# Digits of a packed adjacency taken three to a shift, and an early sum in half-width columns from tile 5

## The reference

```
def layer0(x):                        # GRU over summed messages
    msg = x[src] @ W_msg.T + b_msg + edge_embed[clip(edge_type, 0, 8)]
    m = segment_sum(msg, dst)
    h = gru_cell(m, x, W_ih, W_hh, b_ih, b_hh)
def layer1(x):                        # two mean-aggregation layers
    h = relu(x @ w_self1 + mean_agg(x) @ w_neigh1 + b1)
    y = h @ w_self2 + mean_agg(h) @ w_neigh2 + b2
x1  = layernorm(x + layer0(x))
out = layernorm(x1 + layer1(x1))
```

## Time and profile before

| | us |
|---|---|
| median of 3 runs (783.27 to 784.06) | 783.52 |
| the profiled execution | 783.98 |
| its span | 782.2 |
| PE busy, share of the span | 673.8, 86% |
| DVE busy | 505.3, 65% |
| ACT busy | 272.9, 35% |
| POOL busy | 159.9, 20% |
| mean granted TensorE clock | 0.971 |

### The profile page before, as it was taken

One profiled execution on the slowest core, in us unless ns is written; L12 is line 12 of the kernel. 1 busy time (PEld: TensorE's weight loads), 2 busy tenths in 40 slices (PEclk: granted clock), 3 DMA queues, 4 the chain that ended last, 5 costly groups with the idle time before them and its releaser, 6 DMA issues.

```text
span 782.2 us, 15765 instructions
## 1 busy us (share of the span) xinstructions
PE 673.8 (86%) x3184; PEld 317.7 (41%) x3184; DVE 505.3 (65%) x1614; ACT 272.9 (35%) x701; POOL 159.9 (20%) x339
## 2 busy tenths in 40 slices
PE   2777777777888989999988999967999999999995
PEld 0222222222333433434333444433555555766663
DVE  7999969999899999999997245661111111034434
ACT  3665552223333534544458325451101112100000
POOL 2454324232222222222220002221001111100000
PEclk9999978999999999999999999989999999999998
DMA  5000000000000000000001011101001110121110
GB/s 152 0 0 0 1 0 1 0 0 1 0 1 0 1 1 0 1 1 1 1 0 52 28 34 34 41 15 44 27 14 40 40 40 28 58 70 41 53 45 16
DMA packets 29312, 17.25 MB, mean 22 GB/s; under 512 B 1737, under 2 KB 28101, under 8 KB 29278
## 3 DMA queue, kind: packets, MB, share of 16 engines
q1 hardware_dynamic: 29278, 16.78, 7.3%
HBM read 10.36 MB, written 6.42 MB: 21 GB/s over the span
## 4 chain that ended last, share of the span: by engine, by line
PE 53%; DVE 25%; issue 10%; DVEq 7%; ACT 3%; DMA 1%; POOL 0%; ACTq 0%; POOLq 0%; SPq 0%
DVE S L585 12%; PE PS L938 11%; PE PS L1175 10%; PE PS L867 9%; PE PS L828 5%; DVE D L579 4%; PE PS L1106 3%; DVE digits L574 3%; DVEq L585 2%; PE PS L999 2%; PE PS L1140 2%; DVEq L606 1%; PE PS L1094 1%; PE PS L1095 1%; ACT AT L1217 1%
## 5 line engine op out<-in xcount | busy, mean ns | idle before, releaser
L867 PE MATMUL PS<-S,D 128*128 128x449 bf16 x786 | 222.8, 368 | 61.3 <-DVE S L585 54.4
L585 DVE TENSOR_SCALAR S<-iota_h,src_col,src_w 128x440 bf16<-128x440 f16 x747 | 250.6, 388 | 0.0
L1217 ACT ACTIVATE AT<-digits 128x512 int32 (+5 forms) x200 | 103.7, 519 | 174.1 <-DVE digits L574 174.1
L867 PEld LDWEIGHTS PS<-S,D 128*128 128x128 bf16 x786 | 75.7, 96 | 208.1 <-DVE S L585 184.6
L438 POOL COPY S<-T 128x27 bf16 (+1 forms) x264 | 109.7, 417 | 241.0 <-PE PS L867 227.1
L579 DVE TENSOR_TENSOR D<-iota_t,dst 128x384 bf16<-128x384 f16 x262 | 91.3, 349 | 12.8 <-PE PS L867 12.1
L828 PE MATMUL PS<-AT,xp 128*128 128x512 bf16 x375 | 89.4, 379 | 0.8 <-ACT Cn L1206 0.8
L938 PE MATMUL PS<-AT,x1p 128*128 (+2 forms) x450 | 86.1, 348 | 0.2 <-issue 0.2
L1175 PE MATMUL PS<-xp,AT 128*128 128x384 bf16 (+1 forms) x525 | 85.6, 326 | 0.0
L574 DVE TENSOR_SCALAR digits<-packedT 128x512 int32<-128x512 int32 (+1 forms) x200 | 62.0, 360 | 11.0 <-ACT packedT L1211 9.3
L1175 PEld LDWEIGHTS PS<-xp,AT 128*128 (+2 forms) x525 | 51.5, 98 | 33.9 <-issue 0.3
(11 more groups left out here) (155 smaller groups left out, 620.0 us busy)
## 6 DMA issues: line engine op xcount, KB each, us to landing
slot<-x_rows SPq DMA_DIRECT2D x12, 256.0 KB, 3.0
xstage<-x SPq DMA_DIRECT2D x6, 256.0 KB, 5.3
x_rows<-slot SPq DMA_DIRECT2D x6, 256.0 KB, 2.2
y_rows<-slot SPq DMA_DIRECT2D x6, 256.0 KB, 2.2
res_rows<-slot SPq DMA_DIRECT2D x6, 256.0 KB, 2.5
slot<-res_rows SPq DMA_DIRECT2D x6, 256.0 KB, 2.8
out_rows<-slot SPq DMA_DIRECT2D x6, 256.0 KB, 2.2
slot<-xT SPq DMA_DIRECT2D x3, 256.0 KB, 2.7
```

The lines of the kernel that those rows point to most:

```text
L585: v.tensor_scalar(S[:, u, 0:SPAN], iota_h[:, :], src_col[:, ds(c0 + u, 1)], src_w[:, ds(c0 + u, 1)], ALU.is_equal, ALU.mult).then_inc(sem( ...
L867: mm(PS[:, par, 0:WIDE], ring[:, u, :], S[:, u, 0:WIDE], start=opens and u == 0, stop=last).then_inc(sem("tiles_summed" if last else "item ...
L1217: a.activation(AT[:, f:f + n // P * DIGITS - DIGITS + 1:DIGITS, ds(t * P, w)], digits[:, at:at + n].rearrange("p (g m) -> p g m", m=P)[:, ...
```

## The change

VectorE takes three words a tile in place of eight digits. Word w is the packed integer shifted right by 3w and masked with three fields of 3 bits, at bits 0, 9 and 18. They lie in the bytes 0, 1 and 2 of the int32, shifted in their byte by 0, 1 and 2 bits. So `take_digits` has three operations (shift and mask as before, another constant), with no ring of planes: word w of the next tile is written once all stores of the tile before are done. It is called once a tile, where the first share stood. ScalarE's `store_digits` reads bytes with a step of four: three copies, one for each byte lane, of 3, 3 and 2 digits (3 x 384, 3 x 384, 2 x 384 elements), scaled by 1, 1/2 and 1/4, and a fourth for the 25th source tile (128 elements). Each stores a sum for `count`, and the count of stores in the semaphore goes from 8 to 4 a tile.

TensorE's early sums of the first 2048 columns are cut in eight sums of 256 columns (`early_half`), each over two tiles, 2u + 5 and 2u + 6, in tiles 5 to 20: 12, 12 and 15 matmuls in odd tiles, 12, 12 and 12 in even ones. Two such sums share a bank; `early_agg` counts after the second. The fifth sum of 512 stays as it was. Nothing is changed in the passes after.

```diff
-SHARES = ((0, 1, 2), (3, 4, 5), (6, 7))
-LEAST = len(SHARES)
+LEAST = 3
...
-RING = 4
-PLANES = TURNED + (RING - 1) * MAIN
+WORDS = 3
+LANES = 3
+STORES = LANES + 1
+MASK = sum(((1 << BITS) - 1) << (BITS * WORDS * lane) for lane in range(LANES))
...
-EARLY_CUTS = (0, 7, 13, 19, TILES)
+EARLY_CUTS = (0, 13, TILES)
...
-            def take_digits(t, some):
+            def take_digits(t):
 
                 dve.wait_ge(sem("packedT_in"), t + 1)
-                for f in some:
-                    dve.wait_ge(sem("digits_stored"), t * DIGITS + (f + 1 + DIGITS - RING))
-                    at, n = plane(f)
-                    v.tensor_scalar(digits[:, at:at + n], packedT[:, 0:n], BITS * f, (1 << BITS) - 1, ALU.logical_shift_right,
+                dve.wait_ge(sem("digits_stored"), t * STORES + STORES)
+                for word in range(WORDS):
+                    n = MAIN if word else TURNED
+                    v.tensor_scalar(digits[:, word, 0:n], packedT[:, 0:n], BITS * word, MASK, ALU.logical_shift_right,
                                     ALU.bitwise_and).then_inc(sem("digits_taken"), 1)
...
-                    edge_rows(t + n, (LAG + n) % 2, lambda i: take_digits(t + n - LAG, SHARES[i]))
+                    edge_rows(t + n, (LAG + n) % 2, lambda i: i or take_digits(t + n - LAG))
...
+            def early_half(u, j0, j1):
+
+                pe.wait_ge(sem("digits_stored"), (2 * u + 3) * STORES)
+                if j0 == 0:
+                    pe.wait_ge(sem("x_split"), NC + 1)
+                at = u % 2 * 2 * P
+                for j in range(j0, j1):
+                    for s in range(PARTS):
+                        ins = mm(PS[:, EARLY_BANKS[u // 2], at:at + 2 * P], xp[:, j, s, :], AT[:, j, u * 2 * P:(u + 1) * 2 * P],
+                                 start=(j == 0 and s == 0), stop=(j == TILES - 1 and s == PARTS - 1))
+                if j1 == TILES and u % 2:
+                    ins.then_inc(sem("early_agg"), 1)
+
             def early_piece(t, n):
-                q, r = divmod(t - LAG - 4, 4)
-                if 0 <= q < EARLY:
+                u, r = divmod(t - LAG - 2, 2)
+                if 0 <= u < 2 * EARLY:
                     j0, j1 = EARLY_CUTS[r:r + 2]
-                    early_sum(q, j0 + (j1 - j0) * n // LEAST, j0 + (j1 - j0) * (n + 1) // LEAST)
+                    early_half(u, j0 + (j1 - j0) * n // LEAST, j0 + (j1 - j0) * (n + 1) // LEAST)
...
-            def store_digits(t, w, some=range(DIGITS)):
-                for f in some:
-                    act.wait_ge(sem("digits_taken"), t * DIGITS + f + 1)
-                    at, n = plane(f)
-                    a.activation(AT[:, f:f + n // P * DIGITS - DIGITS + 1:DIGITS, ds(t * P, w)],
-                                 digits[:, at:at + n].rearrange("p (g m) -> p g m", m=P)[:, :, 0:w], ACT.Copy,
-                                 accum_out=count[:, ds(t, 1), f:f + 1].rearrange("p a b -> p (a b)")).then_inc(sem("digits_stored"), 1)
+            def store_digits(t, w):
+                digit_bytes = digits[:, :, :].bitcast(u8).rearrange("p f (g m k) -> p f g m k", m=P, k=4)
+                for lane in range(LANES):
+                    n = min(WORDS, DIGITS - WORDS * lane)
+                    act.wait_ge(sem("digits_taken"), t * WORDS + n)
+                    a.activation(AT[:, 0:TILES - 1, ds(t * P, w)].rearrange("p (g f) m -> p f g m", f=DIGITS)[:, WORDS * lane:WORDS * lane + n, :, :],
+                                 digit_bytes[:, 0:n, 0:GROUPS, 0:w, lane], ACT.Copy, scale=2.0 ** (8 * lane - BITS * WORDS * lane),
+                                 accum_out=count[:, ds(t, 1), lane:lane + 1].rearrange("p a b -> p (a b)")).then_inc(sem("digits_stored"), 1)
+                a.activation(AT[:, TILES - 1, ds(t * P, w)], digit_bytes[:, 0, GROUPS, 0:w, 0], ACT.Copy,
+                             accum_out=count[:, ds(t, 1), LANES:LANES + 1].rearrange("p a b -> p (a b)")).then_inc(sem("digits_stored"), 1)
...
-                    for share in SHARES:
-                        store_digits(t - LAG, P, share)
+                    store_digits(t - LAG, P)
```

More of the change, by code:

```diff
@@ L46 @@
 ROW = WIDE + -WIDE % 4
-RING = 4
-PLANES = TURNED + (RING - 1) * MAIN
+WORDS = 3
+LANES = 3
+STORES = LANES + 1
+MASK = sum(((1 << BITS) - 1) << (BITS * WORDS * lane) for lane in range(LANES))
+assert WORDS * LANES >= DIGITS and BITS * WORDS * LANES <= 27 and MASK < 1 << 24
+assert all(8 * lane <= BITS * WORDS * lane and BITS * WORDS * lane + BITS <= 8 * lane + 8 for lane in range(LANES))
 PAD_DST = 4000
@@ L63, in graph_kernel @@
     fp32, bf16, fp16 = mybir.dt.float32, mybir.dt.bfloat16, mybir.dt.float16
-    i32, u32 = mybir.dt.int32, mybir.dt.uint32
+    i32, u32, u8 = mybir.dt.int32, mybir.dt.uint32, mybir.dt.uint8
     ALU, ACT, AX = mybir.AluOpType, mybir.ActivationFunctionType, mybir.AxisListType
-    SIZE = {fp32: 4, i32: 4, u32: 4, bf16: 2, fp16: 2}
+    SIZE = {u8: 1, fp32: 4, i32: 4, u32: 4, bf16: 2, fp16: 2}
     ds = bass.ds
@@ L99, in graph_kernel @@
     r = [A_at]
-    digits = place(r, "digits", [P, PLANES], i32)
+    digits = place(r, "digits", [P, WORDS, TURNED], i32)
     packedT = place(r, "packedT", [P, TURNED], i32)
@@ L141, in graph_kernel @@
     c_stage = sb("c_stage", [P, 4, NTYPE], fp32)
-    count = sb("count", [P, TILES, DIGITS], fp32)
+    count = sb("count", [P, TILES, STORES], fp32)
     ident = sb("ident", [P, P], fp32)
@@ L263, in general_rows @@
             return call
-        def plane(f):
-            at = f % RING
-            return (TURNED + (at - 1) * MAIN if at else 0, MAIN if f else TURNED)
         def is_dense(t):
@@ L319, in x_load @@
                 if q == 1:
-                    sp.wait_ge(sem("digits_stored"), (TILES + 1) * DIGITS)
+                    sp.wait_ge(sem("digits_stored"), (TILES + 1) * STORES)
                 elif q == 3:
@@ L640, in sum_out @@
                 v.tensor_copy(s_at(q)[:, :], PS[:, bank, :]).then_inc(sem("sums_out"), 1)
-            take_digits(TILES - 3, range(DIGITS))
+            take_digits(TILES - 3)
             dve.wait_ge(sem("tiles_summed"), TILES)
@@ L645, in _ @@
                 sum_out(q)
-            take_digits(TILES - 2, range(DIGITS))
-            take_digits(TILES - 1, range(DIGITS))
-            dve.wait_ge(sem("digits_stored"), (TILES + 1) * DIGITS)
+            take_digits(TILES - 2)
+            take_digits(TILES - 1)
+            dve.wait_ge(sem("digits_stored"), (TILES + 1) * STORES)
             v.tensor_reduce(verdict[:, :], count[:, :, :], AX.XY, ALU.add).then_inc(sem("verdict_set"), 1)
@@ L820, in early_sum @@
             def early_sum(q, j0, j1):
-                pe.wait_ge(sem("digits_stored"), (4 * q + 5) * DIGITS)
+                pe.wait_ge(sem("digits_stored"), (4 * q + 5) * STORES)
                 if j0 == 0:
                     pe.wait_ge(sem("x_split"), NC + 1)
-                bank = EARLY_BANKS[q] if q < EARLY else 0
+                bank = 0
                 for j in range(j0, j1):
@@ L1010, in agg @@
                     between[share]()
-            pe.wait_ge(sem("digits_stored"), (TILES + 1) * DIGITS)
+            pe.wait_ge(sem("digits_stored"), (TILES + 1) * STORES)
             pe.wait_ge(sem("types_ready"), 1)
@@ L1209, in packedT_in @@
                 act.wait_ge(sem("turned"), t + 1)
-                act.wait_ge(sem("digits_taken"), t * DIGITS)
+                act.wait_ge(sem("digits_taken"), t * WORDS)
                 a.activation(packedT[:, :], PS[:, 4, :], ACT.Copy).then_inc(sem("packedT_in"), 1)
-            def store_digits(t, w, some=range(DIGITS)):
-                for f in some:
-                    act.wait_ge(sem("digits_taken"), t * DIGITS + f + 1)
-                    at, n = plane(f)
-                    a.activation(AT[:, f:f + n // P * DIGITS - DIGITS + 1:DIGITS, ds(t * P, w)],
-                                 digits[:, at:at + n].rearrange("p (g m) -> p g m", m=P)[:, :, 0:w], ACT.Copy,
-                                 accum_out=count[:, ds(t, 1), f:f + 1].rearrange("p a b -> p (a b)")).then_inc(sem("digits_stored"), 1)
+            def store_digits(t, w):
[8 more added lines that the diff above has]
+                             accum_out=count[:, ds(t, 1), LANES:LANES + 1].rearrange("p a b -> p (a b)")).then_inc(sem("digits_stored"), 1)
             for c in range(NC + 1):
@@ L1226, in _ @@
                 a.activation(xp[0:rows, 4 * c:4 * c + k, 0, :], xstage[0:rows, 4 * c:4 * c + k, :], ACT.Copy).then_inc(sem("x_hi"), 1)
-            act.sem_inc(sem("digits_stored"), DIGITS)
+            act.sem_inc(sem("digits_stored"), STORES)
             act.wait_ge(sem("keys_set"), 1)
```

## The result

| | before | after |
|---|---|---|
| median of the runs, us | 783.79 (4 runs) | 763.83 (4 runs, 762.49 to 764.25) |
| ratio | | 0.9725, 95% interval 0.9676 to 0.9774 |
| the profiled execution, us | 783.98 | 762.49 |
| its span | 782.2 | 760.7 |
| DVE busy | 505.3 | 469.4 |

The change gains 20 us by the medians; forecast were 18.4, from 783.52 to 765.1. The ratio is that of the means: the fourth execution of the kernel before took 789.83 us, the other three 783.27 to 784.06. This spread belongs to the kernel before. In the series of e11 the gain is 23.4 us (786.79 to 763.4).

What follows compares the result with a forecast made beforehand. VectorE was taken to limit inside tiles, TensorE's gapless 8.10 us chain at edges of tiles with pieces. Loop -17.8 and end -0.8 sum to -18.6, taken as -18.4: 783.52 to 765.1 us, range 757 to 772.

Steps and rivals of the forecast that it cites:

- The bound: Tile loop: VectorE limits only inside a tile; at edges with pieces TensorE's gapless 8.10 us becomes the fixed part.
- Rival 1: Tile loop: VectorE alone limits and TensorE's edges are slack, so 37 us gained, 747 us; chance 0.07.
- The stretches: Loop cut at tile borders, each stretch's gain forecast separately: -17.8 us in all, against 29 us of work removed.
- to h2 of tile 20: From h2 (third half batch) of tile 7, tiles with pieces: 164.0 us becomes 157.9, -6.
- to h0 of tile 24: From h2 of tile 20 to tile 24's first half batch, mostly tiles without pieces: 41.0 us becomes 34.9, -6.1.
- The first term: Tiles 3 and 4, no pieces before or after: VectorE limits, 2 x 1.33 = -2.7 us.
- the low-clock starts of tiles 5 and 7: Tile starts at the lower TensorE clock, assumed to go; if they stay, 1.8 us come back.
- The pieces: TensorE's early-sum matmuls in the loop: 109 ns each at 256 columns, twelve in 1.31 us, weight loads hidden.
- Rival 4: TensorE's early sums: weight loads do not hide behind 256 columns, 207 ns a matmul, +57 us, 822; chance 0.01.
- The byte copies: ScalarE's four stores a tile: 3.6 us for 4.2, reading every fourth byte at the int32 cost an element.
- Rivals 2 and 3: ScalarE's byte stores cost more: 5.4 us a tile, 771.6 us, chance 0.07; or 9.0 us, 797 us, chance 0.03.
- The end: After the loop: last sum some 0.5 us sooner, verdict about 15 us after the last S, short wait gone: -0.8 us.

Runs made afterwards that it cites:

- e11: The changed kernel run again without edits, beside the kernel before on one chip: 763.4 us, ratio 0.9704.
- e7: The changed kernel with twelve more unused 256-column matmuls behind the third piece, between the last batch's halves, in tiles 5 to 20: 785.0 us.
- e8: The changed kernel with twelve more unused 256-column matmuls right behind each tile's first batch, in tiles 5 to 20: 764.57 us.
- e5: The changed kernel with its eight narrow early sums left out but for the last source tile: 740.88 us.
- e1: The changed kernel with the early sums of before put back (512 columns, from tile 7): 763.86 us, ratio 0.9713.
- e4: The changed kernel with nine stores a tile in place of four, reading the same bytes: 765.41 us.
- e6: The kernel before with its four early sums left out but for the last source tile: 785.93 us, ratio 0.9991.
- e12: e6 with four unused 256-column matmuls in each of the two TensorE gaps left by the later digit shares, tiles 3 to 24: 773.42 us.
- e9: The changed kernel with the same early-sum matmuls in five places a tile instead of three: 750.4 us, ratio 0.954.

## Why the prediction was right

**The bound.** The forecast did not take VectorE's 93% as proof that it alone limits; it took TensorE's 8.10 us without a gap as the limit that a shorter VectorE would meet. e7 (21 us for work at the edge), e8 (1 us for it in the middle) and e5 (23 us for leaving the pieces out) show it. Rival 1, 37 us of gain, is refuted by the same runs.

**The stretches.** By the borders above:

| stretch | forecast | measured |
|---|---|---|
| to the start of tile 5 | -2.7 | -3.2 |
| tiles 5 and 6, to h2 of tile 7 | -1.7 | -1.9 |
| to h2 of tile 20 | -6 | -6.45 |
| to h0 of tile 24 | -6.1 | -6.45 |
| to the last S | -1.3 | -1.3 |
| to the copy of the last sum | -0.8 | -1.0 |

The sum to there is -20.4 for -18.6. Each term has its sign and its size; all but one are a little small. The period of a three-batch tile with pieces was forecast at 10.3 and 10.7 us and came at 10.23 and 10.69. That of four batches with fifteen matmuls in the last piece was forecast at 13.0 from h2 to h2 and came at 12.99 in tile 11. Without pieces 9.1 was forecast, and tiles 22 and 23 took 9.13 and 8.92. The digit operations are 75 for 200 and busy for 25.8 us, VectorE's waits for TensorE are 30.0 us, and in the loop the digits wait for nothing, as the forecast had it.

**The first term** is short by half a microsecond since I let the low-clock start of tile 4 stand: tile 3 became 1.26 us shorter and tile 4 1.83, where each was to lose 1.33. The forecast took away only the low-clock starts of tiles 5 and 7 (1.8 us) and, without a word, that of tile 24, where h0 came 2.49 us after the start and was reckoned at 1.87. In the trace of the changed kernel the granted clock falls for the last time at the start of tile 3 and then nowhere in the loop. That the forecast's time came so near is helped by its starting point: 783.52 us is the kernel before near its fastest. Against the 23.4 us gained in the series of e11 the forecast gain of 18.4 is short by 5 us, not by 1.6.

**The pieces.** 109 ns were forecast for 256 columns, 109 measured. The Trainium skill (TensorE: Matmul & The Clock Gate, Back-to-back issue gap) gives 81 ns at 128 columns and 131 at 512 for a sustained stream, and 2.5 ns above the columns' time for a single matmul. The trace agrees with the second figure and not with the first: this is a stream, and it takes 109 ns at 256 columns. Rival 4 is refuted: 600 loads of 98 ns stand beside 600 matmuls at 109 ns spacing, and e1 beside the changed kernel shows that doubling the loads cost nothing. The Trainium skill (the same page, Part 3, The mechanism) has the rule that a weight load overlaps only where the row group differs; the trace disagrees.

**The byte copies.** 3.6 us a tile were forecast; the copies start at 390.25 in tile 24 and packed follows at 393.68, so 3.4. Rivals 2 and 3 fall with it. A copy with a step of four bytes costs no more an element than the int32 copy, 0.85 ns against 0.93. The Trainium skill (SBUF — State Buffer, the note on cachelines) has full bandwidth as long as a 16-byte line is hit at least twice, and a step of four bytes hits it four times; the trace agrees.

**The end.** The last sum started 0.7 us sooner relative to the last S, forecast was 0.5, and the wait for the verdict went. The verdict came sooner than forecast: its reduction starts 13.7 us after the last S, where about 15 were forecast, and a tile's digits and stores there take 5.0 us in series (400.82 to 405.85) and not 5.3. The time that this gives is not gained, since TensorE comes for the verdict only later. e4 shows how near ScalarE is there: 0.93 us more a tile cost 2.0 us.

**What I had wrong** is outside the forecast's sum: the expectation of e6. It took away work of the kernel before without asking what the clock would do with the gaps. Smaller misses are e4, with 2.0 us for 1, and e12, with 12.5 us for 8 to 10. In the forecast itself the clock was worth 1.8 us and 0.6 us, and the reason given there (the idle time around the later digits goes) is what e5, e6 and e12 together bear out. What made the kernel before slower in the later series is not shown; its time goes with its granted clock, but no trace of such an execution was kept.

## What to carry to other kernels

Before cutting the busiest engine's work, follow the chain through one period and find the longest stretch that the other engine fills without a gap: that stretch is the new period's fixed part, whatever the busy shares say. Then look at where the other engine's work stands, not how much it is. Here 20 us came from cutting VectorE's work, and 13 more from placing the same matmuls where TensorE had time between two half batches. That ends where the gapless stretch has become the whole period, as in e9; from there on only less work of TensorE helps.

## What the runs showed of the hardware

- Work that is left out can bring the clock down and cost what it saved: e6 against the kernel before, 785.93 beside 787.5 on the same chip, with a granted clock of 0.88 over tiles 3 to 19. Work that nobody needs can earn it back: e12, with 176 matmuls more than e6, is 12.5 us faster, at a granted clock of 0.99. The matmuls after the idle gaps ran at 1.2 GHz (0.37 us for 449 columns) in e6 and at 2.4 in e12.
- TensorE takes bf16 matmuls of 256 columns, each with 128 x 128 new weights, every 109 ns (15 in 1.64 us in the chain of tile 11), 2 to 3 ns more than its columns at 2.4 GHz.
- ScalarE reads bytes with a step of four at 0.85 ns an element and writes them as bf16, no slower than int32: in e4 a copy of 384 such bytes took 0.51 to 0.52 us, and in the kernel before one of 384 int32 took 0.511.
